# Attention kernel with softmax sums from two accumulators: merging one into the other by a DMA, and moving the sums from step 6 to step 9

## What is computed

```python
xn = layernorm(x)
x = x + attention(xn) + experts(xn)
# attention, per head h of 32:
scores = einsum('qd,kd->qk', q, k) * scale
probs = softmax(scores, axis=-1)
ctx = probs @ v
```

## Time and profile before

| | |
|---|---|
| time, median of 3 runs | 2595.83 us (2594.63 to 2596.72) |
| the profiled execution: time, span | 2596.82 us, 2595.0 us |
| TensorE busy (matmuls) | 2532.0 us, 98% |
| VectorE busy | 1512.7 us, 58% |
| ScalarE busy | 1218.1 us, 47% |
| GpSimd busy | 1607.3 us, 62% |
| queue of GpSimd's DMAs (q0) | 162.54 MB, 32.4% of 16 engines' span |
| queue of SP's DMAs (q1) | 186.70 MB, 25.2% |

### The profile page before, as it was taken

One profiled execution on the slowest core, in us unless ns is written; L12 is line 12 of the kernel. 1 busy time (PEld: TensorE's weight loads), 2 busy tenths in 40 slices (PEclk: granted clock), 3 DMA queues, 4 the chain that ended last, 5 costly groups with the idle time before them and its releaser, 6 DMA issues. The chain is left out here.

```text
span 2595.0 us, 34876 instructions
## 1 busy us (share of the span) xinstructions
PE 2532.0 (98%) x13032; PEld 1648.6 (64%) x13032; DVE 1512.7 (58%) x2522; ACT 1218.1 (47%) x2299; POOL 1607.3 (62%) x529
## 2 busy tenths in 40 slices
PE   7999999999989999999999999999999999979999
PEld 6888888777855555555555555555555555428887
DVE  8511111011658888878878878888888888532222
ACT  3211111111026667666766666666666667750000
POOL 0100111101138999999999999999999999942211
PEclk9999999999989999999999999999999999989999
DMA  4233324222356787787787787787787787633332
GB/s 154 90 122 121 113 110 133 73 73 73 90 154 128 157 169 152 155 169 151 157 165 155 156 166 152 158 166 152 159 164 151 161 167 145 124 107 103 110 111 93
DMA packets 168168, 351.01 MB, mean 135 GB/s; under 512 B 89632, under 2 KB 114720, under 8 KB 137376
## 3 DMA queue, kind: packets, MB, share of 16 engines
q0 software_dynamic: 22320, 162.54, 32.4%
q1 hardware_dynamic: 145712, 186.70, 25.2%
HBM read 122.44 MB, written 63.69 MB: 72 GB/s over the span
## 5 line engine op out<-in xcount | busy, mean ns | idle before, releaser
L991 DVE TENSOR_REDUCE part_max<-ps_b 128x1 f32<-128x512 f32 x1984 | 1213.3, 679 | 276.2 <-PE ps_b L868 276.1
L819 POOL TENSOR_TENSOR psum_p<-psum_p,probs 128x2048 f32<-128x2048 f32 x254 | 1183.5, 4660 | 55.7 <-ACT probs L978 44.3
L978 ACT ACTIVATE probs<-ps_b 128x512 f32<-128x512 f32 x1924 | 973.5, 622 | 366.4 <-PE ps_b L858 363.0
L858 PE MATMUL ps_b<-qp,kp 97*128 97x512 f32 x1344 | 550.5, 413 | 4.6 <-ACT probs L978 4.5
L868 PE MATMUL ps_b<-kp,qp 96*128 96x512 f32 x1344 | 536.9, 401 | 7.1 <-DMA qp<-qk_scr 6.5
L886 PE MATMUL ps_b<-probs,vh 128*32 128x512 f32 x3848 | 466.8, 598 | 0.0
L264 POOL TENSOR_TENSOR wlo<-wraw,whi 128x1024 fp32r<-128x1024 f32 x29 | 69.5, 2399 | 624.5 <-ACT whi L398 624.5
L858 PEld LDWEIGHTS ps_b<-qp,kp 97*128 97x128 f32 x1344 | 251.8, 188 | 233.6 <-issue 135.3
L297 PE MATMUL ps_a<-xhi,whi 128*128 128x512 f32 (+1 forms) x800 | 320.1, 400 | 1.1 <-DVE elo L487 0.9
L297 PE MATMUL ps_a<-xlo,whi 128*128 128x512 f32 (+1 forms) x800 | 317.3, 397 | 0.0
L297 PE MATMUL ps_a<-xhi,wlo 128*128 128x512 f32 (+1 forms) x800 | 317.2, 396 | 0.0
(11 more groups left out here) (97 smaller groups left out, 2004.9 us busy)
## 6 DMA issues: line engine op xcount, KB each, us to landing
psum_q<-probs POOLq DMA_DIRECT2D x155, 1024.0 KB, 7.8
qk<-qk_scr SPq DMA_DIRECT2D x66, 256.0 KB, 7.1
qk_scr<-ehi SPq DMA_DIRECT2D x16, 1024.0 KB, 3.9
qk_scr<-elo SPq DMA_DIRECT2D x16, 1024.0 KB, 6.7
kp<-qk_scr SPq DMA_DIRECT2D x63, 256.0 KB, 4.1
qp<-qk_scr SPq DMA_DIRECT2D x63, 256.0 KB, 7.9
wraw<-wcat SPq DMA_DIRECT2D x29, 512.5 KB, 7.5
craw<-cz_scr SPq DMA_DIRECT2D x16, 768.0 KB, 5.0
```

What stands on the lines that cost most here:

```text
L819: pool.tensor_tensor(acc[:, :], first[:, :], tile(h, t)[:, :], ALU.add).then_inc(pool_done, 1)
L858: pe.matmul(ps[:, n % ST_BANKS, :], kp[s][0:PACK + 1, t * P:(t + 1) * P], qp[s][0:PACK + 1, b * NQ:(b + 1) * NQ], start=True, stop=True).t ...
L978: act.activation(tile(h, t)[:, b * NQ:(b + 1) * NQ], ps[:, n % ST_BANKS, :], ACT.Exp, scale=SCALE).then_inc(exp_done, 1)
L991: dve.tensor_reduce(part_max[hn % 2][:, tn, b:b + 1], ps[:, ring_bank(u), :], AX_X, ALU.max) \
```

## The change

After the add of tile 4 in head h, GpSimd issues one more adding DMA, `merge(h-1)`, which adds the whole of `psum_p` of head h-1 onto `psum_q` of head h-1. It first waits for GpSimd's own last add of head h-1 and for chain 14 of head h-1. TensorE's `sums` reads `psum_q` alone, waits for the merge, and stands at step 9 instead of 6. VectorE's reciprocal goes from step 9 to 13. SP's `invert_sums` is cut in two: the spread stays where it was, the store and reload of the reciprocals come last in the head. In the last head the merge stands behind the same tile 4, which there is the fourth add, since that head's adds begin with tiles 0 and 1 and take tile 3 too.

```diff
--- before.py
+++ after.py
@@ -56,7 +56,8 @@
 RING = 8
 LEAD = 4
 TRANSPOSED_AT = TT - LEAD + 1
-SUMS_AT, RECIPROCAL_AT = 6, 9
+MERGED_AFTER = 4
+SUMS_AT, RECIPROCAL_AT = 9, 13
 
 OUT_KT = KT + Z_BLOCKS
 EARLY = 6
@@ -699,7 +700,11 @@
 
         def chain_count(h, t):
 
-            return 16 * (len(CHAIN_TILES) * (h // 2) + CHAIN_TILES.index(t) + 1)
+            return 16 * ((len(CHAIN_TILES) + 1) * (h // 2) + CHAIN_TILES.index(t) + 1)
+
+        def merged_count(h):
+
+            return 16 * (len(CHAIN_TILES) + 1) * (h // 2 + 1)
 
         def based(h, t):
             return h < LAST and t == BASE_TILE
@@ -745,11 +750,13 @@
                 sp.wait_ge(neg_ready, h)
                 sp.dma_start(qp[s][PACK:PACK + 1, :].bitcast(F32), neg_max[h % 2][:, :]).then_inc(negmax_loaded[s], 16)
 
-            def invert_sums(h):
+            def spread_sums(h):
                 sp.wait_ge(sums_taken, h + 1)
                 for b in range(QB):
                     sp.dma_start(sums_q[b * HD:(b + 1) * HD, :], sums_b[b * HD:b * HD + 1, :]) \
                         .then_inc(sums_spread, 16)
+
+            def spread_reciprocals(h):
                 sp.wait_ge(recip_done, h + 1)
                 sp.dma_start(recip_scr.rearrange("(p c) -> p c", p=P), recip_q[:, :]).then_inc(recip_stored, 16)
                 sp.wait_ge(recip_stored, 16 * (h + 1))
@@ -784,11 +791,13 @@
                     if h + 2 < HEADS:
                         sp.wait_ge(pv_done, TT * h + 4)
                         load_queries(h + 2)
-                    invert_sums(h - 1)
+                    spread_sums(h - 1)
                     if h + 2 < HEADS:
                         load_values(h + 2)
                 if h < LAST:
                     load_negmax(h + 1)
+                if h >= 1:
+                    spread_reciprocals(h - 1)
             store_ctx(LAST - 1)
             store_ctx(LAST)
             for s in range(2):
@@ -834,18 +843,29 @@
                 pool.dma_start(psum_q[h % 2][:, :], tile(h, t)[:, :], accum_op=ALU.add) \
                     .then_inc(chained[h % 2], 16)
 
+            def merge(h):
+                pool.wait_ge(pool_done, pool_count(h, POOL_TILES[-1]))
+                pool.wait_ge(chained[h % 2], merged_count(h) - 16)
+                pool.sem_inc(cleared, 1)
+                pool.dma_start(psum_q[h % 2][:, :], psum_p[h % 2][:, :], accum_op=ALU.add) \
+                    .then_inc(chained[h % 2], 16)
+
             for h in range(HEADS):
                 if h >= 2:
                     normalise(h - 2)
                 if h == LAST:
                     for t in LAST_POOL_TILES[1:]:
                         add(h, t)
+                        if t == MERGED_AFTER:
+                            merge(h - 1)
                     continue
                 for t in POOL_ORDER:
                     if t in CHAIN_TILES:
                         chain(h, t)
                     else:
                         add(h, t)
+                    if t == MERGED_AFTER and h >= 1:
+                        merge(h - 1)
             normalise(LAST - 1)
 
         @block.tensor
@@ -897,10 +917,8 @@
             def sums(h):
                 u = ("sum", h, 0, 0)
                 wait_ring(pe, u)
-                pe.wait_ge(chained[h % 2], chain_count(h, CHAIN_TILES[-1]))
-                sum_of(ring_bank(u), psum_q[h % 2], True, False)
-                pe.wait_ge(pool_done, pool_count(h, POOL_TILES[-1]))
-                sum_of(ring_bank(u), psum_p[h % 2], False, True).then_inc(sum_ready, 1)
+                pe.wait_ge(chained[h % 2], merged_count(h))
+                sum_of(ring_bank(u), psum_q[h % 2], True, True).then_inc(sum_ready, 1)
 
             def last_sums(t):
                 u = ("sum", LAST, 0, 0)
```

## The result

| | before | after |
|---|---|---|
| median of the runs, us | 2596.27 (2594.63 to 2597.19, 4 runs) | 2650.06 (2648.59 to 2658.16, 4 runs) |
| profiled execution, its span, us | 2596.82, 2595.0 | 2651.23, 2649.4 |
| mean granted TensorE clock over the span | 0.992 | 0.983 |
| one head (mean of 29, by ScalarE's copy of the sums) | 48.41 | 50.01 |
| head 31 (by the copy of the sums, which the change moves from step 6 to 9) | 46.82 | 54.01 |

The ratio of after to before is 1.0214, with a 95% interval of 1.0193 to 1.0236. The change costs 54 us, twice what was forecast, and the time lies above the range. Once per head ScalarE copies the finished sums, and once the context, out of PSUM; the distance from one copy to the next is the length of a head.

What follows compares the result with a forecast made beforehand. TensorE was taken to pace the attention stage, GpSimd close behind. +21.7 (heads 1 to 29) - 0.55 (head 30) + 5.8 (head 31) = +27 us on 2595.83 gave 2622.8 us, range 2592 to 2632.

Steps and rivals of the forecast that it cites:

- who goes first: At the DMA engines: already queued query loads precede the merge, or share with it; it lands at 1560.8 to 1561.6.
- TensorE's own 47.89 us: TensorE's period per head if nothing else waits: one group of sums less, one format change more, net -0.55 us.
- B: Rival: merge goes ahead of most queries and lands before TensorE needs it; GpSimd paces; -1.8 us, 2594.0 us; chance 0.17.
- GpSimd's pace: GpSimd's period per head alone: 48.44 less 1.26 us slack plus 0.95 for the merge's issue, 48.13 us.
- C: Rival: besides B, the merge costs GpSimd only 0.61 us, so TensorE paces; -11.5 us, 2584.3 us; chance 0.11.
- D: Rival: GpSimd's DMA queue backs up, chain 9 waits about 1 us; landings 1 us later give 2652 us; chance 0.06.
- heads 1 to 29: Term for heads with query loads: TensorE's wait for the merge outweighs its gain, 29 x 0.75 = +21.7 us.
- head 30: Term for the head without query loads: the merge lands by about 1558 and TensorE gains its 0.55: -0.55 us.
- head 31: Term for the last head: merge behind four adds, TensorE waits 6.7 us and gains 0.86: +5.8 us.
- Behind it stand all scores of step 10: At TensorE's sums in step 9: the 1.3 us wait delays step 10's scores, ScalarE and VectorE, every head.
- Period: 47.89 + 1.3: Head length with TensorE's wait for the merge added: 49.19 us, +0.75 us per head.
- the only wait of a head stands ahead of tile 7: In GpSimd's timeline before the change: its single wait per head, giving 1.26 us of slack.

Runs made afterwards that it cites:

- Run 1: Changed kernel with SP issuing the query loads of head h+2 right behind its key loads, half a head earlier: 2592.74 us, ratio 0.9986.
- run 11: Kernel before the change, with only the query loads issued right behind the key loads, as a control: 2596.96 us, ratio 1.0004.
- run 5: Kernel before, plus the merge's adding DMA into a spare tile nobody reads, reciprocal at step 13 and SP's order split: 2606.17 us, ratio 1.0030.
- run 8: Changed kernel with queries issued right behind the keys and the last merge behind the second of head 31's four adds: 2582.67 us, ratio 0.9947.
- Run 6: Changed kernel with six dummy score matmuls on TensorE ahead of the wait for the merge, in heads 0 to 29: 2635.86 us, ratio 1.0150.
- Run 4: Changed kernel with the last merge, in head 31, behind the second of the four adds instead of the fourth: 2647.12 us, ratio 1.0172.
- runs 3: Kernel before, plus the merge's adding DMA into a spare tile nobody reads, sums and reciprocal where they were: 2650.51 us, ratio 1.0208.
- run 7: Changed kernel with the merge issued one tile earlier, right behind chain 3 (the adding DMA of tile 3): 2610.65 us, ratio 1.0046.

## Why the prediction was wrong

**Right: who goes first, and so the wait.** The merge's place behind the query loads, its landing (11.3 us in the median, within 10.8 to 11.6), TensorE's wait in each head, put down to the adding DMA, and GpSimd's vanished wait at tile 7 came as written. Over heads 1 to 29 TensorE's idle time ahead of the sums is 1.30 us in the mean, just what I took, though in single heads it goes from 0.15 to 2.31. Run 1 shows that the queries make the wait, run 11 that moving the queries gives nothing else, and run 5 that the load without a wait need cost the period nothing (in its profiled execution; its median is 10 us slower). TensorE's own 47.89 us is confirmed by run 1.

**Rivals.** B, the merge ahead of most queries, isn't what the change does. Moving the queries by hand makes its schedule, and then its result, 2594.0 us, comes within 1.3 us of run 1's 2592.74. That is in part luck: GpSimd's pace came out at 48.00 us and not 48.13, some 4 us less over 30 heads, and head 31 has a fall of the clock that B did not have (run 1 is 10 us over run 8, of which the wait is 6.7). C, TensorE paces, is close to that too, since 48.00 is nearly TensorE's 47.89; its reason, a merge at 0.61 us, isn't what was found. D, the backed-up queue, has its wait (1.58 us at chain 9 in the rows above), but GpSimd also waits for ScalarE at tile 4 in most heads, so the backlog alone does not pace them. Landings were not 1 us later, as D's 2652 us needs, so that the measured 2650.06 lies near it is chance.

**Wrong: the price of the wait, and of what hangs on it.** The terms stand beside the copies of the context.

| | forecast | measured |
|---|---|---|
| heads 1 to 29 | +21.7 | +47.0 |
| head 30 | -0.55 | +1.2 |
| head 31 | +5.8 | +6.5 |

- *"Behind it stand all scores of step 10"*, and so *"Period: 47.89 + 1.3"*: this is the step that failed. It priced a wait of TensorE at its own length and nothing more. In heads 1 to 29 the waits ahead of the sums are 39.8 us (37.8 idle, and the 0.07 by which a matmul else overlaps the next), against 29 x 1.3 = 37.7 in the sum: 2.1 more. What the sum lacked is the rest. TensorE works through the stretches at 1.2 GHz, which total 41 us with 1.7 us of idle time in them; that costs half of the remainder, 19.6 us by this estimate (eight matmuls take 1.87 us there instead of 1.00). And the two late loads of the maxima make it stand 3.7 us more. 2.1 + 19.6 + 3.7 = 25.4 us, and 47.0 - 21.7 = 25.3 were missing.
- *Run 6* tests this. With the clock held up, 14.5 of these us come back, though the same merges land as late. It gives less than the 23.3 us of the clock and the late loads, since its fillers and waits together are longer than the waits of after (1.63 us a head over run 1's 47.88, against 1.37). The two heads around 1973 and 2130 us alone are 55.87 + 56.80 - 2 x 49.54 = 13.6 us over the others; the single falls cost 1.6 to 1.7 us each.
- *Head 30* gains its 0.5 us, but the clock falls at the start of head 31, and this costs 1.7.
- *Head 31.* TensorE comes late and waits 4.1 us instead of 6.7, but the clock falls for 10.2 us there. Run 4 puts the wait with all its sequel at 7.35 us, where 6.7 was taken. The mechanism was right, and the size near. Run 1, in which TensorE comes on time, has the wait of the forecast: 6.72 us.

The lower clock was in none of my cases, though the profile of before could have raised the question: its clock is at full level through a stage in which TensorE never stands over 0.36 us, so its rows say nothing of what a wait does to it. What decides whether a wait lowers the clock is not shown by any run. A smaller slip is "the only wait of a head stands ahead of tile 7": a second one, at tile 4, is hidden behind the issue of chain 3, and since it makes GpSimd's slack too small by 0.27 us and the merge costs 0.14 more than I took, the pace of 48.13 us came close to 48.00.

## What to carry to other kernels

An operation that is saved on the pacing engine is paid with a wait, if its input is now a large DMA: compare the landing, behind everything that other queues have already issued, with the moment of need, and leave room for the late ones. Here the remedy was not the merge but three loads from another queue, moved half a head ahead. A wait of 1.4 to 2.3 us on a TensorE that otherwise never stopped cost more than its length here, since the clock fell behind some of them, so such a wait should be priced above its length; and a DMA that nobody waits for can still hold up loads of 2 to 8 KB which somebody does (runs 3 and 5).

## What the runs showed of the hardware that I had not expected

- The granted clock falls to 1.2 GHz behind waits of only 1.44 to 2.31 us (2.13 us at 1577) in a stage where TensorE is otherwise busy without a gap. It doesn't fall behind each (1.64 us at 1527 and 2.19 at 985 left it up), and the time varies with the granted clock from run to run of one kernel (run 4: 2629 to 2662 us). With dummy matmuls in the wait it did not fall in heads 1 to 30 (run 6).
- The landing of an 8 KB load goes from 1.8 to 6.8 us if it is issued 1.8 us behind an adding DMA of 1 MB (after, at 2148), and to 5.9 at 1.4 us behind (after, at 1991).
- Two queues that begin together share the engines packet by packet (34 to 35 packets in 2 us, run 7): the merge lands after 13.7 us instead of 11.3, and the queries after 9.2 instead of 8.2. A DMA that is issued 1.8 to 3.4 us behind three loads of another queue waits for them (109 packets of theirs to none of its data in 2.8 us, in after).
